# Routed tiles in pairs, with the intermediate split in 128 and 64 rows, in a two-layer attention and mixture-of-experts kernel

## What is computed

```python
logits = xf @ router_w.T + router_b            # layer 0: 32 experts, 4 per row; layer 1: 8 experts, 2 per row
top_vals, top_idx = jax.lax.top_k(logits, K)
g = silu(einsum('th,eih->tei', xf, gate_w))    # i: 192 in layer 0, 176 in layer 1
u = einsum('th,eih->tei', xf, up_w)
routed = einsum('tei,ehi,te->th', g * u, down_w, combine)
shared = silu(xf @ sg.T) * (xf @ su.T) @ sd.T
return routed + shared
```

## Time and profile before

| | |
|---|---|
| three runs | 414.17, 413.13, 414.14 us; median 414.14 |
| span of the profiled execution | 410.3 us, 8351 instructions |
| PE matmul busy | 349.8 us (85%) |
| DVE busy | 259.0 us (63%) |
| ACT busy | 203.5 us (50%) |
| POOL busy | 181.1 us (44%) |
| routed tiles of layer 0 | from about 84 to 226 us |
| routed tiles of layer 1 | from about 323 to 381 us |

### The profile page before, as it was taken

One profiled execution on the slowest core, in us unless ns is written; L12 is line 12 of the kernel. 1 busy time (PEld: TensorE's weight loads), 2 busy tenths in 40 slices (PEclk: granted clock), 3 DMA queues, 4 the chain that ended last, 5 costly groups with the idle time before them and its releaser, 6 DMA issues.

```text
span 410.3 us, 8351 instructions
## 1 busy us (share of the span) xinstructions
PE 349.8 (85%) x2427; PEld 203.3 (50%) x2427; DVE 259.0 (63%) x706; ACT 203.5 (50%) x487; POOL 181.1 (44%) x322
## 2 busy tenths in 40 slices
PE   0009776789999999999999979999977799999997
PEld 0008654435545554545545667666553444544355
DVE  2998869645555555555555596999877455555274
ACT  1359445255555555555553146999921455553110
POOL 2000002386676666667653035666610656773100
PEclk9999959999999999999999988999985999999999
DMA  7999994086323322233563579700011222231441
GB/s 233 395 254 336 299 285 124 14 274 172 101 87 95 91 90 92 91 91 91 140 195 129 193 283 283 208 5 1 2 54 51 78 80 88 93 103 52 147 137 51
DMA packets 28298, 57.33 MB, mean 140 GB/s; under 512 B 3806, under 2 KB 12734, under 8 KB 28254
## 3 DMA queue, kind: packets, MB, share of 16 engines
q1 hardware_dynamic: 20110, 37.85, 30.0%
q0 software_dynamic: 6528, 17.83, 14.2%
q10 hardware_dynamic: 1616, 1.11, 0.9%
HBM read 44.72 MB, written 12.06 MB: 138 GB/s over the span
## 4 chain that ended last, share of the span: by engine, by line
PE 70%; DVE 15%; ACT 6%; issue 4%; DMA 2%; POOL 2%; DVEq 0%; SPq 0%; ACTq 0%; POOLq 0%
PE bank L1329 22%; PE bank L1358 14%; PE bank L1340 6%; PE bank L1208 6%; PE bank L1320 4%; PE bank L1407 3%; PE bank L1419 2%; PE bank L1221 2%; DMA x_sb<-x 2%; DVE x_sb L1026 1%; PE bank L1120 1%; PE bank L1175 1%; ACT arena L671 1%; PE bank L1247 1%; ACT xn L549 1%
## 5 line engine op out<-in xcount | busy, mean ns | idle before, releaser
L1329 PE MATMUL bank<-arena,xT 128*64 x272 | 111.2, 491 | 1.1 <-ACT xT L633 1.1
L1332 PE MATMUL bank<-xn,xT 128*64 128x384 f32 (+1 forms) x272 | 111.2, 491 | 0.0
L507 POOL DMA_INDIRECT xg<-m_xn,tab x68 | 66.0, 970 | 61.3 <-PE bank L1320 29.9
L496 POOL DMA_INDIRECT m_ys<-ysb,dest x68 | 68.6, 1009 | 37.1 <-DVE ysb L948 19.8
L1358 PE MATMUL bank<-arena,hT 96*64 (+1 forms) x272 | 70.3, 380 | 2.4 <-DVE hT L934 2.3
L1361 PE MATMUL bank<-xn,hT 96*64 96x256 f32 (+1 forms) x272 | 70.4, 381 | 0.0
L626 ACT ACTIVATE xn<-arena 128x768 f32 (+1 forms) x68 | 56.3, 827 | 21.7 <-issue 21.6
L960 DVE TENSOR_TENSOR hh<-sg,bank 128x192 f32<-128x192 f32 (+1 forms) x71 | 24.8, 349 | 60.9 <-ACT sg L649 60.9
L1358 PEld LDWEIGHTS bank<-arena,hT 96*64 96x64 f32 (+1 forms) x272 | 34.9, 135 | 38.9 <-issue 28.5
L633 ACT ACTIVATE xT<-bank 128x256 f32<-128x256 f32 x71 | 27.2, 383 | 47.9 <-PE bank L1320 47.1
L928 DVE COPY xn<-arena 96x512 f32 (+1 forms) x68 | 29.0, 427 | 23.1 <-issue 23.1
(11 more groups left out here) (187 smaller groups left out, 588.2 us busy)
## 6 DMA issues: line engine op xcount, KB each, us to landing
arena<-w_gu SPq DMA_DIRECT2D x3, 3456.0 KB, 20.1
arena<-w_dn SPq DMA_DIRECT2D x3, 1728.0 KB, 26.3
arena<-m_ys SPq DMA_DIRECT2D x8, 512.0 KB, 5.2
arena<-w_gu SPq DMA_DIRECT2D x2, 1408.0 KB
m_xn<-xn SPq DMA_DIRECT2D x2, 1024.0 KB, 8.8
arena<-m_ys SPq DMA_DIRECT2D x8, 256.0 KB, 3.4
arena<-w_dn SPq DMA_DIRECT2D x2, 704.0 KB
arena<-w_gu SPq DMA_DIRECT2D x1, 1152.0 KB, 9.9
```

The lines of the kernel that those rows point to most:

```text
L496: nc.gpsimd.indirect_dma_start(out=ys_d[L.name], out_offset=bass.IndirectOffsetOnAxis(ap=dest[:, s:s + 1], axis=0), in_=ysb[:, s % BUFS, : ...
L507: nc.gpsimd.indirect_dma_start(out=xg[:, b, :], out_offset=None, in_=xn_d[L.name], in_offset=bass.IndirectOffsetOnAxis(ap=d["tab"][:, s:s ...
L1329: T.matmul(bank[2 + s % 2][0:BLOCK, 0:2 * J2], xT[:, s % 2, c, 0:BLOCK], arena[:, bass.ds(off + c * 2 * J2, 2 * J2)], start=(c == 0), stop ...
L1332: return T.matmul(bank[2 + s % 2][BLOCK:P, 0:2 * J2], xT[:, s % 2, c, BLOCK:P], gu2[:, s % 2, cols], start=(c == 0), stop=(c == C - 1), ti ...
```

## The change

Tiles run in pairs. PE does for pair `p`: both products `gate_up` whole, `down` of the pair before, `turn_h(p)` and `turn_in(p+2)`; so seven transposes stand together where there were two groups of four in two tiles. The intermediate of a tile (192 or 176 columns) is cut into 128 and a tail of 64 or 48 instead of two halves. The tails of the two tiles of a pair share one block of 128 columns, so a pair has three transposes instead of four, and in `down` the tails lie on the upper and the lower 64 rows of the array, each with its two column halves, for two tiles at once. The down weights are laid out to match: 128 rows, then the tail in rows 0 to 63 and once more in rows 64 to 127, loaded by four transfers instead of one. DVE reads four offsets at once and makes six copies of 256 columns for a pair, where there were two copies of 512 columns and two single reads. The product of the odd tile is two instructions. `ht_copy` and `xT_copy` take a pair at a time, 384 and 512 columns wide. POOL sends a result home ten tiles behind the gather instead of seven. The rows of the shared tiles are fetched earlier. Some small buffers share memory, the identity in bfloat16 is gone, and `hh` is cleared at the start. The core of the diff:

```diff
@@ SP @@
-                sp.dma_start(w[0:L.J, :, L.gu:L.stride], w_dn[:, a:b, :]).then_inc(done, 16)
+                first, tail, rest = L.gu, L.gu + H, P - L.J
+                sp.dma_start(w[0:L.J, :, first:tail], w_dn[:, a:b, 0:H]).then_inc(done, 16)
+                sp.dma_start(w[L.J:P, :, first:tail], w_dn[0:rest, a:b, H:2 * H]).then_inc(done, 16)
+                for r in (0, BLOCK):
+                    sp.dma_start(w[r:r + L.tail, :, tail:L.stride], w_dn[rest:L.J, a:b, H:2 * H]).then_inc(done, 16)
...
-                    if L.tiles - BUFS < s + 1 <= L.tiles - BUFS + len(last_work[L.name]):
-                        shared_rows(L, s + BUFS)
+                    if L.tiles <= s + 10 < L.tiles + len(last_work[L.name]):
+                        shared_rows(L, s + 10)
@@ POOL @@
-                ahead = BUFS + 3
+                ahead = 2 * BUFS + 2
@@ ACT @@
+                gu_second(0)
+                xT_copy(0)
+                gu_second(1)
+                for s in range(every_tile):
+                    gate(s)
+                    gu_second(s + 2)
+                    if s == 0:
+                        xT_copy(1)
+                    if s % 2 == 1:
+                        xT_copy(s // 2 + 2)
@@ DVE @@
+                def dn_second(p):
+                    if 2 * p >= L.tiles:
+                        return
+                    _, offs = nc.values_load_multi_w_load_instructions(
+                        d["etab"][0:1, 4 * p:4 * p + 4], engines=(mybir.EngineType.DVE,), min_val=0, max_val=top)
+                    for t in range(2):
+                        s = 2 * p + t
+                        if s >= 2:
+                            dve.wait_ge(m["d_done"], s - 1)
+                        if L is L0 and s == late_tile:
+                            dve.wait_ge(w_late, 2 * LOAD)
+                        r = slice(t * BLOCK, t * BLOCK + L.tail)
+                        for b in range(2):
+                            V.tensor_copy(tails[r, b, :], arena[r, bass.ds(offs[2 * t + b] + L.gu + H, H)])
+                        V.tensor_copy(dn2[:, t, :], arena[:, bass.ds(offs[2 * t + 1] + L.gu, H)]).then_inc(m["dn_second"], 1)
...
+                def ht_copy(p):
+                    dve.wait_ge(m["ht_done"], p + 1)
+                    if p >= 1:
+                        dve.wait_ge(m["d_done"], 2 * p)
+                    n = 2 * P if 2 * p + 1 == every_tile else 3 * P
+                    V.tensor_copy(hT_pair[:, 0:n], bank[1][:, 0:n]).then_inc(m["hT_copied"], 1)
...
+                for p in range(pairs):
+                    for s in range(2 * p, min(2 * p + 2, every_tile)):
+                        product(s)
+                    if p >= 1:
+                        y_copy(2 * p - 2)
+                        y_copy(2 * p - 1)
+                    dn_second(p)
+                    ht_copy(p)
...
@@ PE @@
+                def turn_h(p):
+                    n = len(tiles_of(p))
+                    pe.wait_ge(m["h_ready"], 2 * p + n)
...
+                    for a in range(n + 1):
+                        ins = T.transpose(bank[1][:, a * P:(a + 1) * P], h_pair[:, a * P:(a + 1) * P], ident[:])
+                    ins.then_inc(m["ht_done"], 1)
+
+                def down(p, offs):
+                    pe.wait_ge(m["hT_copied"], p + 1)
...
+                        T.matmul(y[0:BLOCK, 0:H], hT_pair[:, at:at + BLOCK], arena[:, bass.ds(off + L.gu, H)], start=True,
+                                 stop=False, tile_position=(0, 0))
+                        T.matmul(y[BLOCK:P, 0:H], hT_pair[:, at + BLOCK:at + P], dn2[:, t, :], start=True, stop=False,
+                                 tile_position=(0, BLOCK))
+                    for s, off in zip(tiles_of(p), offs):
+                        t = s % 2
+                        y, r = bank[6 + t], slice(t * BLOCK, t * BLOCK + L.tail)
...
+                        T.matmul(y[0:BLOCK, 0:H], hT_pair[r, P:P + BLOCK], tails[r, 0, :], start=False, stop=True,
+                                 tile_position=(t * BLOCK, 0))
+                        T.matmul(y[BLOCK:P, 0:H], hT_pair[r, P + BLOCK:2 * P], tails[r, 1, :], start=False, stop=True,
+                                 tile_position=(t * BLOCK, BLOCK)).then_inc(m["d_done"], 1)
...
+                for p in range(pairs):
+                    for s, off in zip(tiles_of(p), offs):
+                        gate_up(s, off)
+                    after = weights_of(p + 1)
+                    if p == 0:
+                        turn_in(1)
+                    else:
+                        down(p - 1, before)
+                    turn_h(p)
+                    if p + 2 < pairs:
+                        turn_in(p + 2)
+                    before, offs = offs, after
+                down(pairs - 1, before)
```

More of the change, by code:

```diff
@@ L158, in mk_xattn_ffn @@
         v_x = xn[:].rearrange("p t h -> p (t h)")
[L161 to L163 removed]
+        second = {L.name: v_x[:, 0:2 * L.gu].rearrange("p (b w) -> p b w", b=2) for L in (L0, L1)}
+        tails = v_x[:, NT * H - 2 * H:NT * H].rearrange("p (b h) -> p b h", b=2)
+        assert all(2 * L.gu <= NT * H - 2 * H for L in (L0, L1))
         xqT = [b[:].rearrange("p t (k m) -> p t k m", k=C) for b in (xg, ysb)]
@@ L920, in tiles @@
                 top = (L.S + L.E - 1) * L.stride
[L922 to L931, removed]
-                    if s >= 2:
-                        dve.wait_ge(m["d_done"], s - 1)
-                    V.tensor_copy(hT[0:L.J, s % 2].rearrange("p a m -> p (a m)"),
-                                  bank[4 + s % 2][0:L.J, 0:2 * P]).then_inc(m["hT_copied"], 1)
+                every_tile = L.tiles + len(last_work[L.name])
@@ L1365, in tiles, with tiles_of, weights_of @@
-                every_tile = L.tiles + len(last_work[L.name])
-                turn_in(0)
-                before, off = None, weights_of(0)
-                for s in range(every_tile):
-                    pe.wait_ge(m["xT_copied"], s + 1)
+                def tiles_of(p):
+                    return range(2 * p, min(2 * p + 2, every_tile))
+                def weights_of(p):
+                    if p >= pairs:
+                        return None
+                    if 2 * p >= L.tiles:
+                        return [last_work[L.name][s - L.tiles][0] * L.stride for s in tiles_of(p)]
+                    return [pe.value_load(d["etab"][0:1, 2 * s:2 * s + 1], min_val=0, max_val=top) for s in tiles_of(p)]
@@ new lines, in turn_in @@
+                def turn_in(p):
+                    for s in tiles_of(p):
+                        if s < L.tiles:
+                            pe.wait_ge(m["xg_in"][s % BUFS], 16 * (s // BUFS + 1))
+                        else:
+                            pe.wait_ge(m["rows_in"][s % BUFS], 16)
+                        if s % 2 == 0 and p >= 1:
+                            pe.wait_ge(m["xT_copied"], p)
+                        for c in range(C):
+                            at = (s % 2) * H + c * P
+                            ins = T.transpose(bank[0][:, at:at + P], xg[:, s % BUFS, c * P:(c + 1) * P], ident[:])
+                        ins.then_inc(m["t_done"], 1)
@@ L1385, in tiles @@
-                    before, off = off, after
-                turn_h(every_tile - 1)
-                down(every_tile - 1, before)
+                        pe.wait_ge(w_late, 2 * LOAD)
+                    out = bank[2 + s % 2]
+                    for c in range(C):
+                        cols = slice(c * 2 * J2, (c + 1) * 2 * J2)
+                        if s >= L.tiles:
+                            ins = T.matmul(out[:, 0:2 * J2], xT[:, s % 4, c, :], arena[:, off + c * 2 * J2:off + (c + 1) * 2 * J2],
+                                           start=(c == 0), stop=(c == C - 1))
+                            continue
+                        T.matmul(out[0:BLOCK, 0:2 * J2], xT[:, s % 4, c, 0:BLOCK], arena[:, bass.ds(off + c * 2 * J2, 2 * J2)],
+                                 start=(c == 0), stop=(c == C - 1), tile_position=(0, 0))
+                        ins = T.matmul(out[BLOCK:P, 0:2 * J2], xT[:, s % 4, c, BLOCK:P], gu2[:, s % 2, cols],
+                                       start=(c == 0), stop=(c == C - 1), tile_position=(0, BLOCK))
```

220 lines of the change are left out of this document (92 added, 128 removed).

## The result

The changed kernel takes 427.6 us (median of 4 runs, 426.9 to 433.1) against 414.1 of the kernel before: 1.035 times as long [1.031, 1.039]. The forecast was 407.7, range 400 to 422, with faster the likelier side. The profiled execution spans 425.8, so 21.9 is to be explained against the 403.9 (410.3 - 6.4) that the forecast made of the span. What lies around the span is 1.8 us here (427.56 for the run that spans 425.8), and so it is for the kernel before (412.05 for a run that spans 410.3), not 3.8: the profiled execution of before was one of the fastest of its runs, which go from 412.0 to 416.3. So 427.6 is 19.9 above the forecast while the spans are 21.9 apart. The ratios, unlike the medians and ranges, leave out runs that stand well above the others of the same kernel.

A forecast was written before the change was run, and what follows sets the result against it. PE was taken to bound the kernel before, with DVE's chain close behind and deciding the changed pair's period, T = 5.28. 32 x 5.28 - 175.4 = -6.4, so 414.1 - 6.4 = 407.7 us, range 400 to 422.

The forecast's parts named there:

- 3.8: Time by which the median run, 414.14 us, exceeds the profiled execution's 410.3; taken as fixed.
- PE's sum for a pair: PE's work on two tiles: gate records 2.58, down product 1.29, shape change 0.20, transposes 1.07; sum 5.14 us.
- break-even of 5.48: Pair period at which both layers together gain nothing, though a pair took 5.76, because pairs start and end later.
- rival 2: DVE's chain between down products passes 5.48 through offsets and copies; typical 5.7, 421 us; dear checks and copies 5.86, 426; chance 0.25.
- T: Period of a pair in both layers, set by DVE's chain between down products: 5.28 us, between 5.2 and 5.45.
- together at 0.09: Cheap case for DVE's four offset checks: one instruction reads all four, each check 0.09, 0.35 us in all.
- 0.30 each: Dear case for DVE's four offset checks: about 0.30 for each value, 1.2 us in all; 0.95 was taken.
- rival 4: POOL becomes the bound: a home coinciding with a DVE copy takes 1.20 instead of 1.00; some 420 us; chance 0.09.
- 0 to 4.5, I take 2.4: Delay in us of layer 0's first down product by late weights landing while the third to sixth gathers run.
- 93.6: Layer 0's first down product, in us, before the late weights' delay is added; with it 96.0.
- rival 3: On PE, the tails of the two row halves run one after the other; T = 5.71, 421.4 us; chance 0.05.
- Rival 1: DVE's chain is cheap, checks fused; T at the floor, 5.16 in layer 0, 4.95 in layer 1; 402.0 us; chance 0.27.

The follow-up runs named there:

- e6_before_hoist: The kernel before, with each tile's one offset read and checked ahead of the copy of the transposed product; 410.9 us, ratio 0.993.
- e9_half_read: The changed kernel, with the first tile's two offsets read and checked ahead of the products, the second tile's two left in place; 419.3 us, ratio 1.014.
- e2_no_checks: The changed kernel, with the four offsets read in the same place but not compared with their bounds; 406.6 us, ratio 0.977.
- e3_late6: The changed kernel, with layer 0's late weights held back until PE has transposed six tiles instead of one; 422.8 us, ratio 1.025.
- e1_hoist: The changed kernel, with the read of a pair's four offsets and its checks moved ahead of the pair's two products; 402.2 us, ratio 0.972.

## Why the prediction was wrong

The account of the kernel before held: PE without a hole (e6_before_hoist left its period alone). So did PE's sum for a pair: 5.14 forecast, 5.10 measured as soon as DVE was out of the way. The mechanism that decides was named too, DVE's chain from down product to down product, with its order, its places and its break-even of 5.48; that is rival 2, given 0.25. The step that failed is the sum of that chain: the prediction put T at 5.28, below the break-even, and it measured 5.69 and 5.66 in the usual pairs, 5.81 and 5.67 in the mean. Its terms for the six copies and the four checks were too small, and so was the term for the late start. Rival 2 came near these sizes in its dearest case (T = 5.86, 426), but the range was closed at 422.

| term of the chain | forecast | measured at 154.85 to 160.54 |
|---|---|---|
| first down record to `y_copy` | 1.71 | 1.71 |
| to the read | 0.10 | 0.10 |
| read, with its gap | 0.34 | 0.37 |
| four checks, with gaps | 0.95 | 1.13 |
| address, to the first copy | 0.10 | 0.11 |
| six copies | 1.23 | 1.58 |
| `ht_copy` | 0.55 | 0.54 |
| to the down product | 0.30 | 0.15 |
| sum | 5.28 | 5.69 |

- **The copies** are the term with the largest miss, 0.35. A copy does take 0.21 from start to start, but two of the six steps take 0.30, which makes 1.44 (e9_half_read, layer 1), and one copy stretched by a transfer of POOL makes it 1.58. The prediction priced the meeting of a copy and a home as a loss to POOL (rival 4); what it left out is that DVE loses too, and in the chain. No run changed the copies alone: their share is read from the traces.
- **The checks**: 1.13 between "together at 0.09" and "0.30 each" was near the upper bound. The prediction took 0.95, and e2_no_checks shows that without them the period would have been PE's own.
- **Every fourth pair** of layer 0 has 0.48 more and the one behind it 0.18 (read 0.53 instead of 0.34, and others); the mean is 5.81 for that. No run without the four checks in the chain shows the pattern; its cause is open.
- **The start**: 102.3 instead of 96.0. 3.3 is the later first gather: 2.9 go with the clock in the routing stage, by which before's profile had been at the early end, and 0.4 with the change. The other 3.0 come behind it, most of them from the sixth gather, 6.6 us to land beside the late weights, and the half clock behind that hole. The hold of e3_late6 gave back some 4.5 at this place, so "0 to 4.5, I take 2.4" was some 2 too low. The 93.6 that it starts from is itself 0.3 too high: the 12.3 us of layer 1 from second gather to first down product make 93.3.
- **What was right**: the tails run together (rival 3 fell), POOL does not bind (in e1_hoist it works without waits at 2.57 for a tile, 5.14 for a pair, and its lead lasts although PE takes 5.10), and at an equal clock the first gather is only 0.4 later.

The sum: layer 0 has 23 x (5.81 - 5.28) = 12.2, layer 1 has 9 x (5.67 - 5.28) = 3.5, the first down product 6.3; between the layers -1.7 and at the end 1.5 (last down product to the end: 32.1 instead of 30.5), neither of which was traced to a cause. Together 21.8 of the 21.9 in the spans.

Rival 1, the cheap chain, gave 402.0. With the chain made cheap by moving the read, the kernel takes 402.2. That the two agree so closely is luck. The periods were sized well: they are PE's own, 5.10 and 4.89, against the 5.16 and 4.95 of the rival, and the smaller one in layer 1 is what the forecast's single T had not allowed. But the first down product came 2.6 later than the 96.0 (98.6), the stretch behind the last one was 1.6 longer than the forecast's 30.5 (32.1), and what lies around the span is 2.0 less than the 3.8 that the sum took.

## What to carry to other kernels

Where batching puts several small steps of one engine between a producer and its consumer, add them up before counting the gain on the engine that was full: here 0.66 us a pair won on PE was lost on VectorE. A register load whose value was known long before belongs where the engine still has work queued: in e1_hoist its checks occupied the sequencer and not the engine, and 0.28 us for each checked value was nothing there and 1.1 us a pair in the chain. And before a late start is put down to a change, the same window should be read in more than one execution.

## What the runs showed of the hardware that was not expected

- The sequencer of VectorE runs ahead of its engine: in e1_hoist 1.5 us of reading and checking pass under queued copies, with no hole in the engine's timeline.
- A copy between SBUF buffers that is still running as one of POOL's indirect transfers ends takes up to 0.55 us instead of 0.28. In the changed kernel's timelines of DVE and POOL:

```profile
158.77 1.07 POOL L504 DMA_INDIRECT m_ys<-ysb,dest  x1 [0.30 <-issue]
159.00 0.50 DVE L956 COPY xn<-arena 64x256 f32 x2
159.51 0.42 DVE L957 COPY dn<-arena 128x256 f32 x1
```

The transfer ends at 159.84 and the long copy at 159.93. It is so each time: in the changed kernel, e1_hoist and e9_half_read 106 of these copies from 103 us on take 0.38 to 0.55, and every one of them ends 0.09 to 0.12 behind the end of a transfer. A copy that starts 0.2 or less before that end would be done later anyway and keeps its 0.3 (in e9_half_read one starts at 353.96, a gather ends at 354.06). Six copies take 1.43 to 1.55 with none held, 1.54 to 1.72 with one and 1.65 to 1.93 with two, while the transfer itself takes 1.07 instead of 0.99. The kernel before has a meeting of this kind too, with the home that stands in the earlier trace rows with its usual 1.00, from 334.31 to 335.31; its copies of 512 columns take 0.42 as a rule:

```profile
334.91 0.62 DVE L928 COPY xn<-arena 88x512 f32 x1 [0.32 <-issue]
```

The Trainium skill ("SBUF — State Buffer", two separate sides) has an exclusive lock between the two engines, held for the whole instruction of whichever came first. The rows agree for the copy that waits out the transfer's end. The two copies before it (0.50 together) lie wholly inside the transfer's row and are not held, which that rule would not have if the row is the instruction's true extent; spans on POOL are rough.
- A load of four registers took 0.34 us, and each of the two loads of two in e9_half_read 0.53. Why is open.
- A change of the array's shape showed as 0.32 between the last 128-row record and the first tail (155.54 to 155.86), where records of one shape stand 0.21 apart.
